# Deformable sampling on one core: the sum over 24 products moves from one VectorE reduction to a halving on VectorE and four adds on GpSimd, and VectorE makes one of the four one-hot blocks

## The chip, the core and the metric

The kernel runs on one core of a Trainium2 chip. The metric is device time in microseconds (us) of that core. The profile shows one execution; the span is the part of it that the trace covers.

## What is computed

The reference is a hybrid block: a group norm and a projection, a deformable attention over a 16x16 grid, a GEGLU feed-forward, a self-attention and a mixture of experts. The change lies in the sampling step of the deformable attention:

```
v   = value.reshape(bsz, L, NH, d)               # 4 images, L = 256 positions, 8 heads, d = 16
off = (query @ soff_w + soff_b)                  # 8 sample points (NP) per query and head
aw  = softmax(query @ attw_w + attw_b)           # a weight for each point
sampled = bilinear(v, px, py)                    # 4 corners each
out = einsum('bhqpd,bhqp->bqhd', sampled, aw)    # sum over the 8 points
```

## The kernel before, in words

The five engines run their own instruction lists, written by hand, and meet at counting semaphores. There is no planner: the order on an engine is the order of the text.

**Sampling.** For each head `i` (8 of them) and each half `u` of the query positions (2) there is one round, so 16 rounds. Four images are treated at once. In a round:

- `distances(i, u, c)` for c = 0 to 3 on TensorE (PE), line 1259: two matmuls of 512 columns write, for points 2c and 2c+1, a squared distance of each of 128 rows of the value table to the wanted row. Blocks 0 and 2 go to PSUM banks 0 and 1, blocks 1 and 3 to banks 2 and 3.
- `one_hots(i, u)` on ScalarE (ACT), line 574: Relu of one minus that distance turns each block of 1024 columns into a one-hot matrix in bf16 (`hot`). `hot` has a buffer for each u.
- `gather(i, u, b)` for images b = 0 to 3 on PE, line 1275: 24 matmuls of 48 columns each, the one-hot matrices as weights, fetch 8 points x 3 taps x 16 channels into PSUM banks 4 to 7. The first, `gather(i, u, 0)`, waits until all four one-hot blocks of its round are made.
- On VectorE (DVE), line 926: for each pair of images c (0 and 1) a multiplication of 768 columns by the weights `wk3` into `prod`; line 931: a reduction over the 24 products (8 points x 3 taps) of each channel into `msda`.

PE writes the distances of the next round between the gathers of the present one: `distances(next, 0)`, `gather(0)`, `distances(next, 1)`, `gather(1)`, and so on. Rounds run in a loop over heads, two rounds for each turn of the loop, on PE, ACT and DVE; the last head stands behind the loop.

`distances(i, u, c)` waits for the one-hot block that last used its banks. So block 3 waits until block 1 of the same round has been read, and, since PE works in order, everything behind it in PE's list waits as well.

**Ahead of the loop.** PE makes the four distance blocks of the first round in order. ACT makes one-hot block 0, then the exponentials of the softmax (line 587), then blocks 1, 2 and 3. DVE works off a list of its own before its loop: softmax sums, the tap weights `wk3` (line 909), and last the addition of a bias row to `t0_k` (line 913).

**GpSimd (POOL).** Once `wk3` is ready it splits the GEGLU weights and the query and key weights of the attention into a high and a low part: 16 instructions of 256 columns (lines 466 and 469), then one addition over 1024 columns (line 474). Then it has nothing to do until the sampling is over.

**Behind the loop.** PE does `residual()` and then transposes `msda` (line 1311), which waits for the last reductions. All that follows depends on that.

Of the kernel before, what the change touches and what calls it, by code (L numbers as in the profile page):

```python
# [19 lines left out]
P = 128  # L20
# [48 lines left out]
def build(nc, x, weights, vectors, rows, w1_t, w2_t, out):  # L69
    with ExitStack() as ctx:  # L70
        def sb(name, shape, dt=F32):
            return ctx.enter_context(nc.sbuf_tensor(name, shape, dt))
# [37 lines left out]
        sel_low = sb("sel_low", [P, 4, NP])  # L110
        minus_2j = sb("minus_2j", [P, P])

# [9 lines left out]
        def W(name):  # L122
            a, b = WAT[name]
            return w_sb[:, a:b]
# [9 lines left out]
        def tok(name):  # L134
# [70 lines left out]
        prod = hat_y[:, :, :, :].rearrange("q k t r -> q (k t r)").rearrange(  # L205
            "q (s b n d) -> q s b n d", s=2, b=2, d=DH)
        msda = sb("msda", [P, TILES, NH, DH])

# [69 lines left out]
        def sems(names):  # L278
            return [sem(n) for n in names.split()]
# [20 lines left out]
        terms_ready, terms_mm, terms_t_ready, wk3_ready = sems("terms_ready terms_mm terms_t_ready wk3_ready")  # L300
        dist_mm, hot_ready, g_ready, g_free, prod_free = sems("dist_mm hot_ready g_ready g_free prod_free")
        msda_mm, msda_c_ready, out_mm, t1_ready, t1_mm, t1_c_ready = sems(
            "msda_mm msda_c_ready out_mm t1_ready t1_mm t1_c_ready")
        geglu_parted, hn_h_ready, hn_l_ready, wqk_parted, z1_h_ready, z1_l_ready = sems(
# [58 lines left out]
        NMAX_ZEROED, V_ZEROED, ROUTE_ZEROED = 1, 2, 3  # L363
        HOT_CREDIT, G_CREDIT, FREE_CREDIT = 2, 3, 2
        CONSTS = 6
# [46 lines left out]
        def _(pool):  # L412
            nc.gpsimd.memset(one_c[:, :], 1.0)
            nc.gpsimd.memset(ident[:, :], 0.0).then_inc(pool_step, 1)
            nc.gpsimd.memset(group_mean[:, :], GROUPS / C).then_inc(pool_step, 1)
            nc.gpsimd.iota(minus_2j[:, :], pattern=[[-2, P]], base=0, channel_multiplier=0,
                           allow_small_or_imprecise_dtypes=True).then_inc(ramp_ready, 1)
# [39 lines left out]

            pool.wait_ge(ld_wc, 16)
            pool.wait_ge(wk3_ready, NK)
            wqk = w_sb[:, WAT["wq"][0]:WAT["wk"][1]]  # L460
            quarter = 2 * GE * P // 4
            for w, high, low, parted in ((W("geglu"), geglu_h, geglu_l, geglu_parted),
                                         (wqk, wqk_h[:, :], wqk_l[:, :], wqk_parted)):
                for n in range(4):
                    cols = slice(n * quarter, (n + 1) * quarter)
                    nc.gpsimd.tensor_tensor(high[:, cols], w[:, cols], one_c[:, 0:1].to_broadcast([P, quarter]),
                                            ALU.mult).then_inc(parted, 1)
                    pool.wait_ge(parted, 2 * n + 1)
                    nc.gpsimd.tensor_tensor(low[:, cols], w[:, cols], high[:, cols].bitcast(F32),
                                            ALU.subtract).then_inc(parted, 1)  # L470


            pool.wait_ge(fuse_ready, 3)
# [21 lines left out]
        def _(act):  # L495
# [15 lines left out]
            def selectors(which):  # L511
                for n in which:
                    h, p = n // NP, n % NP
                    at = 4 * NP * h + p
                    ins = nc.scalar.activation(sel[:, h, p, :], minus_2j[:, :], ACT.Identity,  # L515
                                               scale=ident[:, at:at + 1], bias=sel_low[:, h, p:p + 1])
                ins.then_inc(sel_ready, 1)
# [48 lines left out]

            def one_hots(i, u, which=range(NP // 2)):

                act.wait_ge(g_ready, 4 * i + 2 * u + 1)
                for c in which:
                    act.wait_ge(dist_mm, 8 * i + 4 * u + c + 1)
                    nc.scalar.activation(hot[:, u, 2 * c:2 * c + 2, :, :],  # L574
                                         ps[:, 2 * (c % 2):2 * (c % 2) + 2, :].rearrange("r p (b q) -> r p b q", b=B),
                                         ACT.Relu, scale=-1.0, bias=one_less_sq[:, 0:1]).then_inc(hot_ready, 1)

# [9 lines left out]
            nc.scalar.activation(aw[:, :, :], aw[:, :, :], ACT.Exp).then_inc(logit_exp, 1)  # L587
            one_hots(0, 0, range(1, 4))

# [152 lines left out]
        def _(dve):  # L742
# [42 lines left out]
            for k in range(NK):  # L785
# [3 lines left out]
            by_term = ident[:, :].rearrange("k (h c p) -> k h c p", h=4, c=4)  # L789
            nc.vector.tensor_tensor(sel_low[:, :, :], by_term[:, :, 1, :], by_term[:, :, 2, :],  # L790
                                    ALU.add).then_inc(sel_low_ready, 1)

# [49 lines left out]
            nc.vector.memset(gap[:, 2:3], 0.0).then_inc(g_free, FREE_CREDIT)  # L842
            nc.vector.memset(gap[:, 3:4], 0.0).then_inc(prod_free, FREE_CREDIT)

# [72 lines left out]

            with dve.Fori(0, NH) as i:
                for u in range(2):
                    for c in range(2):  # L920
                        dve.wait_ge(g_ready, 4 * i + 2 * u + c + 1 + G_CREDIT)

                        dve.wait_ge(prod_free, 4 * i + 2 * u + c + 1)
                        g = ps[:, 4 + 2 * c:6 + 2 * c, 0:NP * NK * DH].rearrange("q b (n d) -> q b n d", d=DH)
                        w = wk3[:, 4 * c + u:4 * c + u + 3:2, bass.ds(i * NP, NP), :].rearrange("q b p k -> q b (p k)")
                        nc.vector.tensor_tensor(prod[:, c, :, :, :], g,  # L926
                                                w.unsqueeze(3).to_broadcast([P, 2, NP * NK, DH]),
                                                ALU.mult).then_inc(g_free, 1)
                    for c in range(2):
                        dve.wait_ge(g_free, 4 * i + 2 * u + c + 1 + FREE_CREDIT)  # L930
                        nc.vector.tensor_reduce(msda[:, 4 * c + u:4 * c + u + 3:2, bass.ds(i, 1), :].rearrange(  # L931
                                                    "q b h d -> q b (h d)"),
                                                prod[:, c, :, :, :].rearrange("q b n d -> q b d n"),
                                                AX_X, ALU.add).then_inc(prod_free, 1)


# [221 lines left out]
        def _(pe):  # L1158
# [509 lines left out]
```

## Time and profile before

| | |
|---|---|
| median of 3 runs | 285.82 us (285.53 to 286.98) |
| the profiled execution's own time | 284.63 us |
| its span | 282.8 us |
| PE busy | 228.8 us (81%) |
| DVE busy | 210.1 us (74%) |
| ACT busy | 177.7 us (63%) |
| POOL busy | 50.0 us (18%) |
| sampling rounds, from the first gather to the last | 39.97 to 113.83 us of the span |

Busy times are sums over the whole span, which has several stages with different limits; what bounds the sampling has to be read inside its own stretch. All times below are us from the start of the span unless marked ns. The page of the profile says of itself that ends of matmuls are modelled and that spans on POOL are rough.

### The profile page before, as it was taken

The numbers are of one execution on the slowest core, as the hardware profiler recorded it, in microseconds if no ns is written. First come the engines' busy times: TensorE is split into PE (matmuls) and PEld (weight loads), VectorE is DVE, ScalarE is ACT, GpSimd is POOL, SyncE is SP. The second block draws the span as 40 slices with busy tenths as digits, with TensorE's granted clock in tenths as the row PEclk, the third lists the DMA queues.
The fourth block names the chain that finished last, engine by engine and source line by source line (L and its number), as shares of the span: only waits on it lengthen the run. The fifth ranks groups of instructions, "written<-read, shape, count | busy, mean of one in ns | idle before, by whom it ended". The sixth has DMA issues, their size and how long they took to land.

```text
span 282.8 us, 7527 instructions
## 1 busy us (share of the span) xinstructions
PE 228.8 (81%) x2908; PEld 158.0 (56%) x2908; DVE 210.1 (74%) x481; ACT 177.7 (63%) x260; POOL 50.0 (18%) x64
## 2 busy tenths in 40 slices
PE   0899469999999998769999568999876605999984
PEld 0579237676767677547989456666544404233352
DVE  4757887999999999874245877888747979697512
ACT  8678979898989897058343567566673232566510
POOL 7004939800000000010002000000000277500000
PEclk9999959999999999987999999999999555799999
DMA  6920000000000000690000000000009515130002
GB/s 144 378 94 2 1 0 2 0 2 0 0 0 0 0 0 2 241 351 4 0 3 0 0 0 2 2 0 2 1 2 370 234 48 163 44 112 2 0 2 74
DMA packets 8836, 16.15 MB, mean 57 GB/s; under 512 B 752, under 2 KB 5104, under 8 KB 8432
## 3 DMA queue, kind: packets, MB, share of 16 engines
q1 hardware_dynamic: 8304, 14.83, 15.0%
q0 software_dynamic: 512, 1.05, 1.2%
q8 instruction: 13, 0.21, 0.3%
q14 instruction: 7, 0.06, 0.1%
HBM read 12.73 MB, written 3.15 MB: 56 GB/s over the span
## 4 chain that ended last, share of the span: by engine, by line
PE 63%; DVE 12%; ACT 9%; issue 7%; DMA 4%; POOL 2%; SPq 1%; POOLq 0%; DVEq 0%; ACTq 0%
PE ps L1275 12%; PE ps L1259 9%; PE ps L1569 8%; ACT arena L574 3%; DVE t_k L972 3%; PE ps L1342 3%; PE ps L1425 2%; PE ps L1374 2%; POOL slot_rows L490 2%; PE ps L1386 2%; PE ps L1588 2%; PE ps L1163 2%; DMA r_sb<-in_rows 2%; PE ps L1332 2%; PE ps L1398 2%
## 5 line engine op out<-in xcount | busy, mean ns | idle before, releaser
L574 ACT ACTIVATE arena<-ps,one_less_sq 128x1024 bf16<-128x1024 f32 x64 | 68.7, 1114 | 7.3 <-PE ps L1259 7.0
L1275 PEld LDWEIGHTS ps<-arena 128*128 128x128 bf16 x1536 | 47.6, 96 | 19.7 <-issue 7.4
L1275 PE MATMUL ps<-arena 128*128 (+1 forms) x1536 | 50.4, 184 | 2.2 <-ACT arena L574 2.1
L1259 PE MATMUL ps<-wide,sel 128*128 (+1 forms) x128 | 39.2, 390 | 8.1 <-ACT arena L574 6.1
L931 DVE TENSOR_REDUCE msda<-wide 128x768 f32 x32 | 45.3, 1458 | 0.0
L926 DVE TENSOR_TENSOR wide<-ps,wide 128x768 f32<-128x768 f32 x32 | 29.8, 955 | 4.0 <-PE ps L1275 4.0
L490 POOL DMA_INDIRECT slot_rows<-nrm,slots x16 | 16.5, 1034 | 72.6 <-DVE slots L1067 68.0
L1569 PE MATMUL ps<-arena,w_sb 128*32 x48 | 23.3, 632 | 0.0
L972 DVE TENSOR_REDUCE t_k<-ps 128x2 f32<-128x512 f32 x32 | 20.5, 683 | 0.0
L643 ACT ACTIVATE wide<-ps 128x512 f32<-128x512 f32 x32 | 17.3, 595 | 1.4 <-PE ps L1410 1.3
L1574 PE MATMUL ps<-late,w_sb 128*32 128x512 f32 x80 | 16.5, 662 | 0.0
L1099 DVE COPY late<-arena 128x512 f32 x40 | 14.2, 425 | 2.2 <-issue 2.2
L947 DVE SCALAR_TENSOR_TENSOR wide<-ps,v_sb,wide 128x512 f32<-128x512 f32 x8 | 6.0, 751 | 12.8 <-ACT wide L616 12.8
L1259 PEld LDWEIGHTS ps<-wide,sel 128*128 (+1 forms) x128 | 8.8, 96 | 11.4 <-ACT arena L574 7.0
L965 DVE SCALAR_TENSOR_TENSOR xm<-ps,raw_by,xm 128x512 fp32r<-128x512 f32 x16 | 11.9, 748 | 3.7 <-ACT xm L632 1.9
L1569 PEld LDWEIGHTS ps<-arena,w_sb 128*32 128x32 f32 x48 | 5.4, 116 | 15.1 <-issue 15.1
L477 POOL MEMSET t_k<- 128x1024 f32 x1 | 1.0, 951 | 67.1 <-PE ps L1315 67.1
L515 ACT ACTIVATE sel<-minus_2j,sel_low,ident 128x128 bf16<-128x128 f32 x32 | 12.6, 479 | 0.0
L635 ACT ACTIVATE xm<-ps,high_by 128x512 fp32r<-128x512 f32 x8 | 5.5, 687 | 10.5 <-PE ps L1374 10.5
L737 ACT ACTIVATE sel<-ps 128x512 f32<-128x512 f32 x12 | 7.2, 598 | 7.0 <-PE ps L1574 7.0
L616 ACT ACTIVATE wide<-ps,v_sb 128x512 f32<-128x512 f32 x8 | 5.5, 691 | 8.6 <-PE ps L1332 8.6
L1163 PE MATMUL ps<-ident,nrm 128*128 128x128 f32 x32 | 8.5, 368 | 2.5 <-DVE nrm L777 2.5
(298 smaller groups left out, 497.3 us busy)
## 6 DMA issues: line engine op xcount, KB each, us to landing
arena<-in_w_t SPq DMA_DIRECT2D x1, 4096.0 KB, 15.0
wide<-in_w_t SPq DMA_DIRECT2D x1, 2048.0 KB, 8.0
slot_rows<-t_c SPq DMA_DIRECT2D x2, 768.0 KB, 9.9
wide<-in_w_t SPq DMA_DIRECT2D x1, 1536.0 KB, 11.3
late<-slot_rows SPq DMA_DIRECT2D x6, 256.0 KB, 3.6
w_sb<-in_weights SPq DMA_DIRECT2D x1, 1480.0 KB, 8.3
x_sb<-in_x SPq DMA_DIRECT2D x4, 128.0 KB, 2.3
wide<-in_w_t SPq DMA_DIRECT2D x1, 512.0 KB, 8.0
```

The lines of the kernel that those rows point to most:

```text
L490: nc.gpsimd.indirect_dma_start(out=scratch[h], out_offset=bass.IndirectOffsetOnAxis(ap=slots[:, c, t:t + 1], axis=0), in_=nrm[:, t, :], in ...
L574: nc.scalar.activation(hot[:, u, 2 * c:2 * c + 2, :, :], ps[:, 2 * (c % 2):2 * (c % 2) + 2, :].rearrange("r p (b q) -> r p b q", b=B), ACT ...
L643: nc.scalar.activation(prob_t[u % 2][:, i, :], ps[:, 2 + i % 2, :], ACT.Exp).then_inc(prob_ready, 1)
L926: nc.vector.tensor_tensor(prod[:, c, :, :, :], g, w.unsqueeze(3).to_broadcast([P, 2, NP * NK, DH]), ALU.mult).then_inc(g_free, 1)
L931: nc.vector.tensor_reduce(msda[:, 4 * c + u:4 * c + u + 3:2, bass.ds(i, 1), :].rearrange("q b h d -> q b (h d)"), prod[:, c, :, :, :].rear ...
L972: nc.vector.tensor_reduce(nmax[:, :, 2 * (u % 2) + i // 2, HROWS * (i % 2) + SPLIT], ps[:, i % 2, :].rearrange("q (t k) -> q t k", t=2), A ...
L1099: nc.vector.tensor_copy(staged_at[n % len(staged_at)], w1_sb[:, bass.ds(at[q][t % GROUP], 1), :].rearrange("d e f -> d (e f)")).then_inc(s ...
L1163: nc.tensor.transpose(ps[:, bank + t // 4, P * (t % 4):P * (t % 4) + P], nrm[:, t, :], ident[:, :]).then_inc(s["turned"], 1)
L1259: ins = nc.tensor.matmul(ps[:, 2 * (c % 2) + p % 2, :], sel[:, bass.ds(i % 4, 1), p, :].rearrange("k h j -> k (h j)"), terms_t[:, bass.ds( ...
L1275: ins = nc.tensor.matmul(ps[:, 4 + b, p * NK * DH:(p + 1) * NK * DH], hot[:, u, p, b, :], rhs, start=(s == 0), stop=(s == PARTS - 1))
L1569: nc.tensor.matmul(ps[0:GRAIN, 2 + t % 4, :], x_cols[:, t * P:t * P + GRAIN], w1_sb[:, bass.ds(at[j], 1), :].rearrange("d e f -> d (e f)"))
L1574: ins = nc.tensor.matmul(ps[GRAIN * q:GRAIN * (q + 1), 2 + t % 4, :], x_cols[:, t * P + GRAIN * q:t * P + GRAIN * (q + 1)], staged_at[entr ...
```

## The change

1. **Sum.** The reduction over 24 products is gone. DVE adds the two halves of each product (12 and 12) at once behind its multiplication, `halve(i, u, c)`, into a new buffer `part_sums`, which has a part for each u. GpSimd adds the remaining twelve down to one in four additions over all four images, `sums(step)`: 384, 192, 64 and 64 columns.
2. **Second one-hot block.** ACT makes blocks 0, 2 and 3 only. DVE makes block 1 from PSUM with one instruction (add, then maximum with 0), `second_one_hot`. For the first round this stands behind DVE's whole list ahead of the loop; in the rounds it stands ahead of the multiplications. To make it one such instruction, the distances come with the opposite sign (`twice_j` in place of `minus_2j`, the sign of `sel_low` turned).
3. **Order on GpSimd.** The 16 weight splits are parted: one ahead of the sums of each round.
4. **Waits.** `distances` of block 3 and `gather` of image 0 wait on the new semaphore `second_hot`; `gather` of image 0 waits for ACT's blocks as well. DVE's one-hot waits until both halvings of the round before are done. The final transposes wait for GpSimd's last sums.

```
-            for w, high, low, parted in ((W("geglu"), ...), (wqk, ...)):
-                for n in range(4):
-                    nc.gpsimd.tensor_tensor(high[:, cols], w[:, cols], one_c[:, 0:1].to_broadcast([P, quarter]), ALU.mult)
-                    pool.wait_ge(parted, 2 * n + 1)
-                    nc.gpsimd.tensor_tensor(low[:, cols], w[:, cols], high[:, cols].bitcast(F32), ALU.subtract)
+            def sums(step):
+                i, u = step // 2, step % 2
+                part = part_sums[:, u, :, :, :]
+                pool.wait_ge(halved, 2 * step + 2 + HALVED_CREDIT)
+                nc.gpsimd.tensor_tensor(part[:, :, 0:6, :], part[:, :, 0:6, :], part[:, :, 6:12, :], ALU.add)
+                pool.wait_ge(sum_step, 3 * step + 1)
+                nc.gpsimd.tensor_tensor(part[:, :, 0:3, :], part[:, :, 0:3, :], part[:, :, 3:6, :], ALU.add)
+                pool.wait_ge(sum_step, 3 * step + 2)
+                nc.gpsimd.tensor_tensor(part[:, :, 0, :], part[:, :, 0, :], part[:, :, 1, :], ALU.add)
+                pool.wait_ge(sum_step, 3 * step + 3)
+                nc.gpsimd.tensor_tensor(msda[:, u:u + 7:2, i, :], part[:, :, 0, :], part[:, :, 2, :],
+                                        ALU.add).then_inc(sums_ready, 1)
+            for step in range(2 * NH):
+                part_weights(step)
+                sums(step)
...
-            def one_hots(i, u, which=range(NP // 2)):
+            def one_hots(i, u, which=(0, 2, 3)):
...
-            one_hots(0, 0, range(1, 4))
+            one_hots(0, 0, (2, 3))
...
             dve.wait_ge(wk3_ready, NK)
-            with dve.Fori(0, NH) as i:
-                for u in range(2):
-                    for c in range(2):
-                        (multiply pair c)
-                    for c in range(2):
-                        nc.vector.tensor_reduce(msda[...], prod[:, c, :, :, :] as "q b d n", AX_X, ALU.add)
+            def second_one_hot(i, u):
+                dve.wait_ge(g_ready, 4 * i + 2 * u + 1)
+                dve.wait_ge(dist_mm, 8 * i + 4 * u + 2)
+                nc.vector.tensor_scalar(hot[:, u, 2:4, :, :], ps[:, 2:4, :], one_less_sq[:, 0:1], 0.0,
+                                        ALU.add, ALU.max).then_inc(second_hot, 1)
+            def halve(i, u, c):
+                dve.wait_ge(g_free, 4 * i + 2 * u + c + 1 + FREE_CREDIT)
+                nc.vector.tensor_tensor(part_sums[:, u, 2 * c:2 * c + 2, :, :], prod[:, c, :, 0:n, :],
+                                        prod[:, c, :, n:2 * n, :], ALU.add).then_inc(halved, 1)
+            def weighted(i, u, last):
+                (wait for both halvings of the round before)
+                second_one_hot(next round)
+                weigh(i, u, 0)
+                dve.wait_ge(sums_ready, 2 * i + u + 1)
+                halve(i, u, 0)
+                weigh(i, u, 1)
+                halve(i, u, 1)
+            second_one_hot(0, 0)
...
             def distances(i, u, c):
-                pe.wait_ge(hot_ready, 8 * i + 4 * u + c + 1)
+                if c == 3:
+                    pe.wait_ge(second_hot, 2 * i + u + 2)
+                else:
+                    pe.wait_ge(hot_ready, 6 * i + 3 * u + c + 1)
...
                 if b == 0:
-                    pe.wait_ge(hot_ready, 8 * i + 4 * u + 4 + HOT_CREDIT)
+                    pe.wait_ge(hot_ready, 6 * i + 3 * u + 3 + HOT_CREDIT)
+                    pe.wait_ge(second_hot, 2 * i + u + 2)
...
-                    pe.wait_ge(prod_free, 4 * NH + FREE_CREDIT)
+                    pe.wait_ge(sums_ready, 2 * NH + SUM_CREDIT)
```

## Rows read from the trace of the kernel before

**Rows 1.** Costliest groups: line, engine, tiles, count | busy us, mean ns | idle before.
```profile
L574 ACT ACTIVATE arena<-ps,one_less_sq 128x1024 bf16<-128x1024 f32 x64 | 68.7, 1114 | 7.3 <-PE ps L1259 7.0
L1275 PE MATMUL ps<-arena 128*128 (+1 forms) x1536 | 50.4, 184 | 2.2 <-ACT arena L574 2.1
L931 DVE TENSOR_REDUCE msda<-wide 128x768 f32 x32 | 45.3, 1458 | 0.0
L926 DVE TENSOR_TENSOR wide<-ps,wide 128x768 f32<-128x768 f32 x32 | 29.8, 955 | 4.0 <-PE ps L1275 4.0
```

**Rows 2.** Busy times by stretch: at the start, and one turn of the loop.
```profile
core 0: us, PE busy (x) PEld busy (x) DVE busy (x) ACT busy (x) POOL busy (x), PEclk, DMA share, GB/s
40.00:42.80 2.80, 2.80 (x49) 2.21 (x50) 2.62 (x4) 1.66 (x2) 1.11 (x1) 0.51 0.00 0
...
78.86:88.29 9.43, 9.02 (x210) 6.62 (x209) 9.04 (x9) 8.58 (x9) 0.00 (x0) 1.00 0.00 0
```

**Rows 3.** Chain that ended last, in order of time, 82 to 93 us.
```profile
82.22 1.12 ACT arena L574
83.34 0.12 issue
83.46 0.77 PE ps L1275 x24
84.23 0.43 PE ps L1259 x2
84.66 0.60 PE ps L1275 x24
...
87.33 0.23 issue
...
91.64 1.12 ACT arena L574
```

**Rows 4.** Timeline of one round: start us, us, engine, line.
```profile
83.01 0.96 DVE L926 TENSOR_TENSOR wide<-ps,wide 128x768 f32<-128x768 f32 x1 [0.39 <-PE ps L1275]
...
84.70 3.18 ACT L574 ACTIVATE arena<-ps,one_less_sq 128x1024 bf16<-128x1024 f32 x3 [0.27 <-PE ps L1259]
...
86.14 0.59 PE L1259 MATMUL ps<-wide,sel 128*128 x2
```

**Rows 5.** Timeline of the start of the rounds.
```profile
36.37 3.34 ACT L574 ACTIVATE arena<-ps,one_less_sq 128x1024 bf16<-128x1024 f32 x3
...
37.52 1.03 PE L1259 MATMUL ps<-wide,sel 128*128 128x512 bf16 x2 [2.34 <-ACT arena L574]
...
39.97 1.31 PE L1275 MATMUL ps<-arena 128*128 x24
...
41.43 1.20 DVE L913 TENSOR_TENSOR t_k<-t_k,fused 128x1024 f32<-128x1024 f32 x1
...
41.69 1.41 POOL L466 TENSOR_TENSOR xm<-w_sb,one_c 128x256 fp32r<-128x256 f32 x1 [4.47 <-DVE wide L909]
```

**Rows 6.** DVE groups near in kind to the new ones, shapes kept apart.
```profile
L965 DVE SCALAR_TENSOR_TENSOR xm<-ps,raw_by,xm 128x512 fp32r<-128x512 f32 x16 | 11.9, 748 | 3.7 <-ACT xm L632 1.9
...
L878 DVE TENSOR_TENSOR arena<-ps,arena 128x384 f32<-128x384 f32 x4 | 2.0, 546 | 0.4 <-ACT arena L557 0.4
```

**Rows 7.** PE's sequencer on the gather's line: count, ns min/median/max.
```profile
L1275 PEldq FUSED_REGOPS  x84: 46/46/70, 39.8 to 100.6; - x84
```

**Rows 8.** Two-input additions and the like on POOL, shapes kept apart.
```profile
L466 POOL TENSOR_TENSOR wqk_h<-w_sb,one_c 128x256 fp32r<-128x256 f32 x4 | 2.5, 616 | 0.0
...
L469 POOL TENSOR_TENSOR xm<-w_sb,xm 128x256 fp32r<-128x256 f32 x4 | 2.9, 729 | 0.3
...
L449 POOL TENSOR_TENSOR hat_x<-hat_x,t_k 128x512 f32<-128x512 f32 x1 | 1.3, 1269 | 0.1
```

**Rows 9.** Timeline of the end of the rounds.
```profile
111.26 2.57 PE L1275 MATMUL ps<-arena 128*128 128x48 bf16 x96 [0.61 <-ACT arena L574]
...
119.05 1.09 PE L1311 MATMUL ps<-ident,msda 128*128 128x128 f32 x8 [1.63 <-DVE msda L931]
```

**Rows 10.** Timeline at 31 us: DVE and POOL both read SBUF.
```profile
30.67 1.92 POOL L446 TENSOR_SCALAR wide<-y_rest 128x512 f32<-128x512 f32 x1
...
31.41 0.69 DVE L887 TENSOR_TENSOR aw<-proj,lmax 128x512 f32<-128x512 f32 x1
```

More of the change, by code:

```diff
@@ L514, in selectors @@
                     at = 4 * NP * h + p
-                    ins = nc.scalar.activation(sel[:, h, p, :], minus_2j[:, :], ACT.Identity,
+                    ins = nc.scalar.activation(sel[:, h, p, :], twice_j[:, :], ACT.Identity,
                                                scale=ident[:, at:at + 1], bias=sel_low[:, h, p:p + 1])
@@ L575, in one_hots @@
                                          ps[:, 2 * (c % 2):2 * (c % 2) + 2, :].rearrange("r p (b q) -> r p b q", b=B),
-                                         ACT.Relu, scale=-1.0, bias=one_less_sq[:, 0:1]).then_inc(hot_ready, 1)
+                                         ACT.Relu, bias=one_less_sq[:, 0:1]).then_inc(hot_ready, 1)
             act.wait_ge(val_r1, B)
@@ L789, in _ @@
             by_term = ident[:, :].rearrange("k (h c p) -> k h c p", h=4, c=4)
-            nc.vector.tensor_tensor(sel_low[:, :, :], by_term[:, :, 1, :], by_term[:, :, 2, :],
-                                    ALU.add).then_inc(sel_low_ready, 1)
+            nc.vector.scalar_tensor_tensor(out=sel_low[:, :, :], in0=by_term[:, :, 1, :], scalar=-1.0,
+                                           in1=by_term[:, :, 2, :], op0=ALU.mult, op1=ALU.subtract).then_inc(sel_low_ready, 1)
             for b in range(B):
@@ new lines, in second_one_hot, with weigh @@
+            def second_one_hot(i, u):
+                dve.wait_ge(g_ready, 4 * i + 2 * u + 1)
+                dve.wait_ge(dist_mm, 8 * i + 4 * u + 2)
+                nc.vector.tensor_scalar(hot[:, u, 2:4, :, :],
+                                        ps[:, 2:4, :].rearrange("r p (b q) -> r p b q", b=B),
+                                        one_less_sq[:, 0:1], 0.0, ALU.add, ALU.max).then_inc(second_hot, 1)
+            def weigh(i, u, c):
+                dve.wait_ge(g_ready, 4 * i + 2 * u + c + 1 + G_CREDIT)
+                g = ps[:, 4 + 2 * c:6 + 2 * c, 0:NP * NK * DH].rearrange("q b (n d) -> q b n d", d=DH)
+                w = wk3[:, 4 * c + u:4 * c + u + 3:2, bass.ds(i * NP, NP), :].rearrange("q b p k -> q b (p k)")
+                nc.vector.tensor_tensor(prod[:, c, :, :, :], g,
+                                        w.unsqueeze(3).to_broadcast([P, 2, NP * NK, DH]),
+                                        ALU.mult).then_inc(g_free, 1)
@@ new lines, in halve @@
+            def halve(i, u, c):
+                n = NP * NK // 2
+                dve.wait_ge(g_free, 4 * i + 2 * u + c + 1 + FREE_CREDIT)
+                nc.vector.tensor_tensor(part_sums[:, u, 2 * c:2 * c + 2, :, :], prod[:, c, :, 0:n, :], prod[:, c, :, n:2 * n, :],
+                                        ALU.add).then_inc(halved, 1)
+            def weighted(i, u, last):
+                if u == 0:
+                    dve.wait_ge(halved, 4 * i + HALVED_CREDIT)
+                else:
+                    dve.wait_ge(halved, 4 * i + 2 + HALVED_CREDIT)
+                if u == 0:
+                    second_one_hot(i, 1)
+                elif not last:
+                    second_one_hot(i + 1, 0)
+                weigh(i, u, 0)
[3 more added lines that the diff above has]
+                halve(i, u, 1)
@@ L937, in _ @@
+            second_one_hot(0, 0)
+            with dve.Fori(0, NH - 1) as i:
+                for u in range(2):
+                    weighted(i, u, False)
+            for u in range(2):
+                weighted(NH - 1, u, True)
             norm(lns["ln3"], 2, out_mm)
```

58 lines of the change are left out of this document (30 added, 28 removed).

## The prediction

> **What bounds the sampling now.** I read four views: the costliest groups, the busy times of one turn of the loop, the chain that ended last, and the timeline at both ends of the rounds. By the groups, DVE's reduction and ACT's one-hots look like the price of this stage [rows 1]; both are what the change lightens. The busy times of one turn (two rounds, 9.43 us) do not choose between them: PE 9.02, DVE 9.04, ACT 8.58 [rows 2]. The chain does [rows 3]. In 82 to 93 us it holds PE's work, PE's issue, and one ACT piece in each turn; DVE stands nowhere in it. The reader is to see three things there.
>
> First, a round with the ACT piece: the last distances of a round end, ACT starts one-hot block 3 at once (82.22), 1.12 us, 0.12 us of issue, and the gather starts at 83.46. ACT isn't late there: it starts as soon as PE has delivered. That block 3 is 1.12 us long counts; how many blocks ACT made before it doesn't. Second, if that wait were gone, PE would in the same place have a gather and a pair of distances to do, 0.60 + 0.43 = 1.03 us in the chain. The wait costs 1.24 - 1.03 = 0.21 us each turn. Third, the other round of the turn is PE alone, with 0.23 us of issue at the loop's end (87.33).
>
> DVE waits 0.39 us for PE once in a turn [rows 4]. It is nearly full but behind PE, not ahead of it. Only at the end is it late: the last gather ends at 111.26 + 2.57 = 113.83, and the transposes wait for the last reduction until 119.05 [rows 9].
>
> **ACT makes three blocks, not four.** 16 instructions of 1114 ns go [rows 1], 17.8 us of ACT. By the chain, what is left on the path is block 3 behind the last distances, and it stays. I take 0. The bound on the other side is PE with no wait at all: 0.21 x 8 = 1.7 us gained.
>
> **DVE's work in a round.** Removed: two reductions, 2 x 1.458 = 2.92 us. Added: two halvings of 384 columns. The same size from PSUM and SBUF took 0.546 [rows 6]; two are 1.09. Added too: block 1, 1024 columns from PSUM with a per-partition scalar. The slope is (955 - 546) / 384 = 1.065 ns a column [rows 1, 6]. L965, with such a scalar, is 748 ns at 512 columns [rows 6], so its fixed part is 748 - 545 = 203 ns, and block 1 is 1.09 + 0.20 = 1.29 us. ACT's 1.11 is the lower bound. A round on DVE goes from 2.92 + 1.91 = 4.83 to 1.29 + 1.91 + 1.09 = 4.29 us of instructions, 0.54 less. Hidden behind PE it is worth 0.
>
> **Is block 1 in time?** This is what DVE now owes PE. Count from the gather at 83.46. The second distances are there when ACT starts at 84.70; the fourth start at 86.14 [rows 4], and behind them stand the rest of PE's list. DVE's multiplication started at 83.01 and ends at 83.97. With hand-overs of 0.1 (the chain's issue is 0.12) the halving ends at 84.62, block 1 runs from 84.72 to 86.01, and PE has it at 86.11. That is in time by 0.03 us; with shorter hand-overs by 0.15. So 0 for this, but without reserve: each 0.1 us later costs 1.5 us over 15 rounds.
>
> **One wait more.** The first gather of a round waits on a second semaphore against a loop value. PE's sequencer takes 46 ns for such an operation [rows 7]. In the chain the gather follows its wait at once, so I add 0.04 x 15 = 0.6 us; the bounds are 0 and, at 0.12 each, 1.8.
>
> **The first round.** Here lies the price. ACT made block 1 of round 0 first in its group of three at 36.37, and PE started the fourth distances at 37.52 and the first gather at 39.97, 2.45 us later [rows 5]. DVE now makes this block, behind L913, which ends at 41.43 + 1.20 = 42.63 [rows 5]. Nothing in DVE's list ahead of it gets shorter or goes. Block 1 is then done at 42.63 + 1.29 = 43.92, and the fourth distances start at 43.95 or a little later: 6.4 us later than 37.52. Behind them in PE's list are the distances of round 1 and all gathers, so the first gather moves from 39.97 to 46.4. ACT's block 3 of round 0 waits for the same distances and ends before PE needs it. Nothing covers this: PE's first round in the trace follows its own pace, and the path through the rounds is PE's. I take +6.4, with 6.2 (block at ACT's duration) to 6.6. In the time before, TensorE ran at 1.2 GHz (granted 0.51) in 40.0 to 42.8, and at 2.4 GHz in the loop [rows 2], after having stood idle for 2.34 us ahead of 37.52 among others. It will now be idle longer, and it may stay at the lower level somewhat further into the rounds: 0 to 1.5 us more; I take 0.
>
> **GpSimd.** Its adds have 384, 192, 64 and 64 columns. From 729 ns at 256 and 1269 at 512 columns [rows 8], 2.11 ns a column and 0.19 fixed: 1.00 + 0.59 + 0.32 + 0.32 = 2.24 us, with four hand-overs of 0.1 about 2.65. One weight split is 0.62 to 0.73 [rows 8]. Together 3.3 us in a round of 4.7: it keeps up and has two buffers. The splits end later than now, but before the feed-forward that reads them, and the addition over 1024 columns behind them still ends ahead of its reader, PE's output of the feed-forward.
>
> **The end.** The last gather ends at G = 113.83 (unshifted). Multiplication 0.96, hand-over, halving 0.55: G + 1.7 = 115.5. GpSimd had the round before since about 112.4 (1.15 us behind the gather at 111.26, as counted above; the last round has no distances and takes 2.57 us): its sums 2.65 and a split 0.73 hold it to 115.8, or 116.3 if a halving holds it up. Then 2.65 us and a hand-over: transposes at 118.5 to 119.0 against 119.05 [rows 9]. I take -0.3.
>
> The turned sign costs nothing: `sel_low` and the ramp stay one instruction each, far ahead of their readers. The load of the expert weights, which SP starts behind the last gather, moves with the whole and is read much later.
>
> **Sum.** 6.4 + 0.6 - 0.3 = +6.7. The profiled execution, 284.63 before, should be about 291.3; the median of the runs shown lies 1.2 us above it, so 285.82 + 6.7 = 292.5.
>
> **Two engines on one memory.** A GpSimd instruction that began at 41.69 under L913, which has two SBUF inputs, took 1.41 us [rows 5] where 0.62 is usual [rows 8]; it ended 0.47 us behind L913. So the halving, also with two SBUF inputs, will hold GpSimd up, 2 x 0.55 us in a round at most, which fits: 3.3 + 1.1 = 4.4. The other way round, L887 with two SBUF inputs ran 0.69 us inside a GpSimd instruction of 1.92 us [rows 10] and wasn't held up: by the slope, 512 columns are 0.54 us and 0.14 fixed. The Trainium skill (SBUF — State Buffer, Who interferes with whom) says that whichever starts second blocks fully until the first has ended. Our trace agrees for GpSimd behind DVE and doesn't for DVE behind GpSimd at L887; by that rule the halvings would be held up too, and the sum would be that of the second case below.
>
> **The cases.**
> (1) Forecast, 0.62: start +6.4, rounds unchanged, 290.5 to 294.5.
> (2) Halvings are held up by GpSimd's adds, 0.18. The adds run from about 1.2 us behind the gather's start for 3.3 us, so the first halving, at 3.4, meets them. Held up by half an instruction to a whole one, 0.3 to 1.0 us, it pushes the second multiplication, the second halving and block 1, which has no reserve: 0.1 to 0.4 us a round, 1.5 to 6 us, 294 to 299. For it: the row at 41.69 shows that the two do collide. Against: L887.
> (3) ACT's relief does help, 0.10: the wait of 0.21 in each turn goes, with the best end: 6.4 - 1.7 - 0.6 = +4.1, 289.9; with part of the start hidden, 288.
> (4) The other side, 0.06: DVE, not PE, sets the pace. Then each round is 0.54 shorter, 8.6 us, against 6.4 at the start: 283.6. It decides from 0.4 us a round on. DVE's 9.04 of 9.43 speaks for it; that it waits 0.39 for PE and is in no piece of the chain, against.
> (5) The lower clock lasts longer, 0.04: 294 to 296.
>
> The range 289 to 298 leaves out the far ends of (2) and (3), and (4). A measurement of this kernel tells 0.5% (1.4 us) from no change. Slower by more: (1), (2), (5) and nearly all of (3), 0.92; faster 0.05; within 0.03.
>
> **What the changed profile would show.** Right: PE idle from about 36 to 43.9 waiting for DVE's block 1 in front of the fourth distances; first gather near 46.4; turns of the loop at 9.4 to 9.5 us; ACT with 3 blocks and over 2 us idle a turn; DVE's one-hot near 1.3 us; four adds and a split of 3.3 us on GpSimd; transposes about 5 us behind the last gather. Wrong: a first gather before 43 us; turns of 8.9 us or less (case 4), or of 9.7 and more with PE waiting for DVE's one-hot in front of the fourth distances (case 2); halvings clearly over 0.55 us.

## The result, and the profile after

The changed kernel takes 299.59 us (median of 4 runs, 297.49 to 299.77), the kernel before 285.67 us beside it (4 runs): ratio 1.0453, 95% interval 1.0397 to 1.051. Slower, as forecast, but by 13.9 us where 6.7 were forecast, and outside the range of 289 to 298. Measured again (f3), the changed kernel came out at 298.25 us (ratio 1.0365, 1.0297 to 1.0432). Ratios leave out runs more than 1.5% above the fastest of the same kernel, which show a lower granted clock; in e4 and g2 most runs are such, the profiled ones too, so these two have no ratio.

The profiled execution took 299.55 us, its span is 297.8: 15.0 more than before. First the costliest groups of the page (line, engine, tiles, count, busy us, mean ns, idle before), to be read against [rows 1, 6, 8].

```profile
L600 ACT ACTIVATE arena<-ps,one_less_sq 128x1024 bf16<-128x1024 f32 x48 | 52.6, 1112 | 31.9 <-PE ps L1318 31.9
...
L1318 PE MATMUL ps<-wide,sel 128*128 (+1 forms) x128 | 39.9, 398 | 13.3 <-DVE arena L950 8.2
...
L959 DVE TENSOR_TENSOR wide<-ps,wide 128x768 f32<-128x768 f32 x32 | 30.4, 951 | 1.1 <-PE ps L1335 1.0
L950 DVE TENSOR_SCALAR arena<-ps,one_less_sq 128x1024 bf16<-128x1024 f32 x16 | 20.5, 1283 | 10.4 <-PE ps L1318 10.4
L482 POOL TENSOR_TENSOR wide<-wide 128x384 f32<-128x384 f32 x16 | 16.0, 998 | 32.2 <-DVE wide L967 32.2
...
L967 DVE TENSOR_TENSOR wide<-wide 128x384 f32<-128x384 f32 x32 | 19.1, 598 | 2.2
```

The new instructions have about the forecast sizes: one-hot on DVE 1.283 us, first add on GpSimd 0.998. ACT's relief has become 31.9 us of idle time. And PE's distances now waited 8.2 us for DVE's one-hot, in one place. The timeline of that place, the changed kernel, against [rows 5]:

```profile
42.06 1.20 DVE L941 TENSOR_TENSOR t_k<-t_k,fused 128x1024 f32<-128x1024 f32 x1
43.19 1.27 DVE L950 TENSOR_SCALAR arena<-ps,one_less_sq 128x1024 bf16<-128x1024 f32 x1
44.52 1.89 PE L1318 MATMUL ps<-wide,sel 128*128 128x512 bf16 x4 [8.23 <-DVE arena L950]
...
47.07 1.34 PE L1335 MATMUL ps<-arena 128*128 x24 [0.66 <-ACT arena L600]
```

The fourth distances stand behind 8.23 us of waiting, and the first gather is at 47.07 instead of 39.97. The chain of a turn in the rounds, the changed kernel, against [rows 3]:

```profile
82.48 0.77 PE ps L1335 x24
...
85.32 0.52 PE ps L1318 x2
85.83 0.60 PE ps L1335 x24
...
87.22 0.12 issue
87.35 0.97 PE ps L1335 x24
...
90.86 1.12 ACT arena L600
...
92.10 0.77 PE ps L1335 x24
```

A turn is 92.10 - 82.48 = 9.62 us where it was 9.43. Two pieces are new in kind: 0.12 us of issue ahead of the gather at the loop's start, and fourth distances of 0.52 us where a pair takes 0.43. What stands ahead of these, by the timeline of the changed kernel:

```profile
83.81 1.28 DVE L950 TENSOR_SCALAR arena<-ps,one_less_sq 128x1024 bf16<-128x1024 f32 x1 [0.25 <-PE ps L1318]
...
85.23 0.60 PE L1318 MATMUL ps<-wide,sel 128*128 x2
```

DVE had waited 0.25 us for PE's second distances before it began block 1, and PE began the fourth distances 0.14 us behind its end. The timeline of the end, the changed kernel, against [rows 9]:

```profile
119.58 0.61 POOL L470 TENSOR_TENSOR wqk_h<-w_sb,one_c 128x256 fp32r<-128x256 f32 x1
...
119.59 1.02 DVE L967 TENSOR_TENSOR wide<-wide 128x384 f32<-128x384 f32 x1
...
120.49 2.57 PE L1335 MATMUL ps<-arena 128*128 128x48 bf16 x96 [0.61 <-ACT arena L600]
...
123.16 0.56 DVE L967 TENSOR_TENSOR wide<-wide 128x384 f32<-128x384 f32 x1
...
123.22 0.95 POOL L485 TENSOR_TENSOR wide<-wide 128x192 f32<-128x192 f32 x1
...
128.51 1.09 PE L1371 MATMUL ps<-ident,msda 128*128 128x128 f32 x8 [1.85 <-POOL msda L490]
```

The transposes start at 128.51, 9.46 us later than the 119.05 of before. That leaves 15.0 - 9.46 = 5.5 us that arise behind the sampling, in stages that the diff does not touch. The busy times by stretch show two of them; the columns are those of [rows 2]. Changed kernel: the attention, and the expert stage.

```profile
163.43:210.84 47.41, 40.27 (x333) 30.17 (x331) 36.45 (x71) 28.67 (x50) 1.91 (x3) 0.89 0.00 1
...
252.68:283.92 31.24, 29.05 (x238) 8.91 (x241) 20.90 (x61) 15.78 (x28) 3.57 (x4) 0.94 0.12 35
```

Kernel before, the same two stretches:

```profile
153.66:198.55 44.89, 36.57 (x332) 27.20 (x331) 36.28 (x71) 28.68 (x50) 1.91 (x3) 1.00 0.00 1
...
240.67:268.88 28.21, 28.21 (x237) 8.68 (x240) 20.71 (x60) 16.15 (x28) 3.43 (x4) 0.94 0.13 39
```

The attention runs at a granted clock of 0.89 instead of 1.00: the same matmuls keep PE busy for 40.27 us instead of 36.57, and the stage takes 2.5 us longer. TensorE was at 1.2 GHz from 174.6 on for 10.2 us. The expert stage is 3.0 us longer with the mean clock unchanged (0.94), but the low stretch lies elsewhere: before, it is at the start of the stage (240.67 to 244.1); in the changed kernel nearly all of it comes later, from 259.9 to 263.3. Ahead of that, ACT and DVE stand still for over 3 us, by the timeline of the changed kernel:

```profile
256.14 0.60 ACT L753 ACTIVATE w_sb<-ps 128x512 f32<-128x512 f32 x1 [3.66 <-remote]
...
259.13 2.77 DVE L1155 COPY late<-arena 128x512 f32 x8 [3.39 <-remote]
```

"Remote" means that the profile saw no instruction of this core that released them.

### The profile page after: what moved, and what is told of

It is laid out like the page before. It is cut to its first block, busy times and chain, and to the rows that moved or that the text cites. A ratio compares the mean times of both kernels' runs of the same rounds, so it can differ in the third digit from the quotient of the medians.

```text
span 297.8 us, 7579 instructions
## 1 busy us (share of the span) xinstructions
PE 236.4 (79%) x2908; PEld 164.8 (55%) x2908; DVE 206.1 (69%) x499; ACT 161.1 (54%) x244; POOL 88.8 (30%) x128
## 4 chain that ended last, share of the span: by engine, by line
PE 63%; DVE 14%; ACT 10%; issue 5%; POOL 2%; another core or an unknown queue 2%; DMA 2%; SPq 1%; DVEq 1%; ACTq 0%
PE ps L1335 12%; PE ps L1318 8%; PE ps L1629 6%; ACT arena L600 4%; DVE t_k L1028 3%; PE ps L1434 3%; PE ps L1402 2%; PE ps L1219 2%; PE ps L1485 2%; PE ps L1446 2%; PE ps L1648 2%; PE ps L1458 2%; DMA r_sb<-in_rows 2%; PE ps L1392 1%
## 5 line engine op out<-in xcount | busy, mean ns | idle before, releaser
L600 ACT ACTIVATE arena<-ps,one_less_sq 128x1024 bf16<-128x1024 f32 x48 | 52.6, 1112 | 31.9 <-PE ps L1318 31.9
L1335 PEld LDWEIGHTS ps<-arena 128*128 128x128 bf16 x1536 | 48.5, 97 | 20.1 <-issue 9.4
L1335 PE MATMUL ps<-arena 128*128 (+1 forms) x1536 | 51.2, 185 | 3.5 <-ACT arena L600 2.8
L950 DVE TENSOR_SCALAR arena<-ps,one_less_sq 128x1024 bf16<-128x1024 f32 x16 | 20.5, 1283 | 10.4 <-PE ps L1318 10.4
L482 POOL TENSOR_TENSOR wide<-wide 128x384 f32<-128x384 f32 x16 | 16.0, 998 | 32.2 <-DVE wide L967 32.2
L967 DVE TENSOR_TENSOR wide<-wide 128x384 f32<-128x384 f32 x32 | 19.1, 598 | 2.2
L1318 PEld LDWEIGHTS ps<-wide,sel 128*128 (+1 forms) x128 | 9.8, 97 | 17.5 <-DVE arena L950 9.1
L541 ACT ACTIVATE sel<-twice_j,sel_low,ident 128x128 bf16<-128x128 f32 x32 | 12.6, 479 | 0.0
L780 DVE BATCH_NORM_STATS2 ln_st<-ps 128x6 f32<-128x128 f32 x24 | 5.3, 283 | 10.1 <-PE ps L1375 6.9
L1434 PE MATMUL ps<-z_h,wqk_h 128*128 128x256 f32 x32 | 11.4, 356 | 0.0
```

Source lines behind the costliest of these rows:

```text
L482: nc.gpsimd.tensor_tensor(part[:, :, 0:6, :], part[:, :, 0:6, :], part[:, :, 6:12, :], ALU.add).then_inc(sum_step, 1)
L600: nc.scalar.activation(hot[:, u, 2 * c:2 * c + 2, :, :], ps[:, 2 * (c % 2):2 * (c % 2) + 2, :].rearrange("r p (b q) -> r p b q", b=B), ACT ...
L950: nc.vector.tensor_scalar(hot[:, u, 2:4, :, :], ps[:, 2:4, :].rearrange("r p (b q) -> r p b q", b=B), one_less_sq[:, 0:1], 0.0, ALU.add, A ...
L967: nc.vector.tensor_tensor(part_sums[:, u, 2 * c:2 * c + 2, :, :], prod[:, c, :, 0:n, :], prod[:, c, :, n:2 * n, :], ALU.add).then_inc(halv ...
L1318: ins = nc.tensor.matmul(ps[:, 2 * (c % 2) + p % 2, :], sel[:, bass.ds(i % 4, 1), p, :].rearrange("k h j -> k (h j)"), terms_t[:, bass.ds( ...
L1335: ins = nc.tensor.matmul(ps[:, 4 + b, p * NK * DH:(p + 1) * NK * DH], hot[:, u, p, b, :], rhs, start=(s == 0), stop=(s == PARTS - 1))
```

## The experiments

Each was run beside the kernel before, and a ratio compares it with that; the kernel before itself took 287.0 us beside e1 to e4, 288.64 beside f1 to f4 and 288.24 beside g1 to g3 (medians; one run of 719.49 us, beside g1 to g3, is out of all ratios). Beside the time I read three marks of each profile: the first gather, the transposes, and what is left of the span behind the transposes. The first two give the price in the sampling; the third tells what came from elsewhere.

**e1: the first round's block 1 back on ACT.** The rounds keep the change.

```diff
 ACT, ahead of one_hots(0, 0, (2, 3)):
+    act.wait_ge(dist_mm, 2)
+    nc.scalar.activation(hot[:, 0, 2:4], ps[:, 2:4], ACT.Relu, bias=one_less_sq).then_inc(second_hot, 1)
 DVE, ahead of its loop:
-    second_one_hot(0, 0)
```

> One-hot block 1 of round 0 alone goes back to ScalarE; all else as in the changed kernel. Theory A (the start): the first gather returns from 47.1 to about 40.0 us, the turns of the loop stay at 9.62 us, the transposes of msda come at about 120.7 (119.05 before, plus 0.2 us for each of 7 turns); if the 5.5 us lost behind the transposes were a consequence of the late start they go too and the time is 286.5 to 288; if they belong to the new code they stay and it is 291 to 293. Rival B (the rounds themselves, VectorE's one-hot and GpSimd's sums, make the cost): the time stays above 294.

290.19 us, ratio 1.015 (1.0095 to 1.0204). First gather 40.47, transposes 121.43, so 6.60 and 7.08 us ahead of the changed kernel's. One edit at one place holds most of the price in the sampling. The turn stays at 9.63 us.

**e2: the sums alone.** As e1, and ACT makes block 1 in every round; the second wait stays.

```diff
-    def one_hots(i, u, which=(0, 2, 3)):
+    def one_hots(i, u, which=(0, 1, 2, 3)):
+        ready = second_hot if c == 1 else hot_ready
 DVE:
-    second_one_hot(next round)
```

> ScalarE makes all four one-hot blocks again; only the halvings, GpSimd's sums and the parted weight splits remain. Theory A: the first gather near 40.0 us, turns of 9.43 to 9.5 us (TensorE and the fourth block set the pace, VectorE has 3.0 us of work in a round of 4.7), transposes at 118.5 to 119.2, time 285 to 287. Rival C (GpSimd and VectorE in each other's way on SBUF lengthen the rounds): turns of 9.6 us or more, 288 or more.

287.51 us (10 runs), ratio 1.0026 (0.9981 to 1.0071), level with the kernel before and not faster. First gather 40.87, transposes 120.80, turn 9.54 us. In its chain the fourth distances take 0.43 us again, and the 0.12 us of issue is still there; the chain of e2:

```profile
88.20 0.43 PE ps L1319 x2
...
90.02 0.12 issue
90.15 0.97 PE ps L1336 x24
```

**e3: the one-hot alone.** As e1, but DVE sums by its old reductions and GpSimd splits the weights in one piece.

```diff
-    halve(i, u, c) and GpSimd's sums(step)
+    nc.vector.tensor_reduce(msda[...], prod[:, c], AX_X, ALU.add)   # c = 0, 1
```

> VectorE makes block 1 of each round but the first (that one on ScalarE) and reduces over 24 products as in the kernel before; GpSimd does the weight splits in one piece at the start. Work of VectorE in a round by instructions: 1.29 + 1.91 + 2.92 = 6.1 us, less 0.3 of overlap. Theory A: VectorE becomes the bound, a turn takes about 11.6 us, the time is 300 to 306. Rival D (what bounds the round is ScalarE's four blocks): turns of 9.4 us or less.

310.94 us (one run), a turn of about 12.7 us where 11.6 had been expected. The timeline of e3 shows why:

```profile
74.37 1.27 DVE L952 TENSOR_SCALAR arena<-ps,one_less_sq 128x1024 bf16<-128x1024 f32 x1
...
75.78 0.60 PE L1319 MATMUL ps<-wide,sel 128*128 x2 [1.72 <-DVE arena L952]
```

PE waits 1.72 us for DVE's block, and DVE in turn waits for PE behind it (17.38 us busy of 20.00). So the two parts of the change are not independent: the sums are what makes room for the one-hot on DVE.

**e4: the kernel before, started late.** An unused memset of 0.91 us on DVE, at the place of the new one-hot, holds back the fourth distances of the first round.

```diff
+    nc.vector.memset(late[:, 0:1024], 0.0).then_inc(dve_consts, 1)   # ahead of DVE's loop
 def distances(i, u, c):
+    if c == 3:
+        pe.wait_ge(dve_consts, 3)
```

> The kernel before, in which TensorE's fourth distances of round 0 wait until VectorE has done the t0_k addition (L913) and one memset of 1024 columns behind it: a late start and nothing else. Theory A: first gather about 6.2 us later, at 46.2; turns stay 9.43. What it tells: if the lower TensorE clock at the start and the loss of 5.5 us behind the transposes follow from the late start, the time is 294 to 299; if they don't, it is 291.5 to 293. Rival B (the rounds make the cost): at most 293 too, so that the rounds would have to show the rest.

297.69 us (median of 4; the fastest 292.47, against 285.33 for the fastest of before beside it). The timeline of e4 shows the changed kernel's start with the old code:

```profile
43.19 0.91 DVE L918 MEMSET late<- 128x1024 f32 x1 [0.16 <-issue]
...
46.61 1.32 PE L1276 MATMUL ps<-arena 128*128 x24 [0.56 <-ACT arena L574]
...
126.65 1.09 PE L1314 MATMUL ps<-ident,msda 128*128 128x128 f32 x8 [1.63 <-DVE msda L932]
```

The transposes are 7.6 us later than before: 6.64 from the start, 0.94 from a first round of 6.72 us instead of 5.78, at a mean granted clock of 0.63 instead of 0.76. The attention of this kernel is slow as well; the busy times of e4:

```profile
161.73:209.47 47.74, 39.40 (x332) 29.06 (x331) 36.38 (x71) 28.67 (x50) 1.91 (x3) 0.93 0.00 1
```

So the slow attention needs no line of the change. It doesn't always come with the late start either: the fastest run of e4, at a mean clock of 0.924 where the profiled one had 0.896, is 7.1 us above the fastest of before, about what the later transposes alone give.

**f1, f2: TensorE filled with useless matmuls ahead of the fourth distances,** in the changed kernel (f1: 12 and 24) and in the one before (f2: 12 and 7). This was to show whether the idle time at the start brings the low clock.

```diff
+    def fill(n):
+        for k in range(n):
+            nc.tensor.matmul(ps[:, 4 + k % 4, :], sel[:, 0, 0, :], terms_t[:, 0, 0:HALF])
 def distances(0, 0, c):
+    if c == 2: fill(12)
+    if c == 3: fill(24)      # 7 in f2
```

> The changed kernel, with 36 matmuls of 512 columns without use on TensorE in the time in which it waits ahead of the rounds (12 in front of the third distances, 24 in front of the fourth), so that it isn't idle there. The late start stays. Theory E (the lower clock in the first rounds follows from the idle time ahead of them): the granted clock stays near 1.00 from 36 to 52, the first gather comes at 46 or a little earlier, the first round is about 4.8 us and not 6.6, gain 1.5 to 2.5 us: 295 to 298. If the low stretch at 174 to 185 us, in the attention, hangs on that idle time too, it goes and 2.5 us more with it. Rival: the low stretches hang on nothing ahead of the rounds; the gain is the first round alone.

> The kernel before with 19 such matmuls in its own two waits ahead of the rounds (12 and 7). Theory E: the clock stays up, the first round takes about 4.8 us in place of 5.78, the start of the gathers isn't later than 40.0: 0.5 to 1.5 us faster than before. Rival: VectorE, whose own list ends at 42.6, holds the first rounds back and nothing is gained, or the matmuls delay the fourth distances: same to 1 us slower.

f1: 300.09 us, ratio 1.0426 (1.0367 to 1.0485): nothing gained. The timeline of f1 shows the second filling and what PE did next:

```profile
35.59 5.34 PE L1361 MATMUL ps<-wide,sel 128*128 128x512 bf16 x24
...
44.43 1.89 PE L1318 MATMUL ps<-wide,sel 128*128 128x512 bf16 x4 [3.49 <-DVE arena L950]
```

The busy times of f1 at the start, in two neighbouring stretches:

```profile
34.00:43.90 9.90, 5.96 (x27) 2.46 (x26) 8.44 (x12) 4.01 (x5) 5.13 (x3) 1.00 0.00 0
...
43.90:50.00 6.10, 4.70 (x54) 2.79 (x56) 1.26 (x2) 2.12 (x2) 0.00 (x0) 0.54 0.00 0
```

The filling was too short: it ended at 40.93, PE then stood idle for 3.49 us until DVE's block was there, and the clock, 1.00 until then, fell to 1.2 GHz at 44.3. The first round took 6.44 us (6.59 in the changed kernel). The attention is at 47.49. So f1 doesn't test a start without idle time. f2 does: there PE never waited longer than 1.0 us ahead of the rounds, and the clock stayed at 1.00 through the whole first round, which took 4.79 us instead of 5.78. f2 took 289.31 us, ratio 1.0046 (1.0003 to 1.0089), not the 0.5 to 1.5 us less that were expected: what is left behind the transposes is 166.7 us against 163.8 before, with 3.4 us at 1.2 GHz in its attention.

**f3: the changed kernel again,** beside f1, f2 and f4.

> The changed kernel once more, unchanged, for its spread and its low stretches of the clock. If the loss of 5.5 us behind the transposes belongs to it, the times are again 297 to 300 and the profile again has a stretch at the lower clock in the attention (170 to 190 us); if it was chance, some executions come at 292 to 294.

298.25 us. First gather 46.99, transposes 128.34, attention 47.42; but the expert stage 29.6 instead of 31.24.

**f4: all weight splits ahead of all sums** on GpSimd; else the changed kernel.

```diff
 for step in range(2 * NH):
     part_weights(step)
+for step in range(2 * NH):
     sums(step)
```

> The changed kernel with all 16 weight splits on GpSimd ahead of the first sums, as before, in place of one ahead of the sums of each round. Theory A: GpSimd keeps up with or without them, they cost nothing in the rounds: turns of 9.62 us as in the changed kernel, same time within 1 us; at the end the last sums no longer stand behind a split, 0.3 to 0.8 us gained there. Rival C (GpSimd's reads lengthen VectorE's halvings and through them the rounds): turns go to 9.5 us or less, 1 us or more faster.

296.32 us, ratio 1.0282 (1.0231 to 1.0333), 1.9 us less than f3. Turns stay at 9.6 to 9.7 us. The transposes are at 127.58, 0.76 ahead of f3's; the attention had the full clock, by the busy times of f4:

```profile
162.22:207.08 44.86, 36.55 (x333) 27.19 (x331) 36.28 (x71) 28.66 (x50) 1.91 (x3) 1.00 0.00 1
```

All four runs of f4 have a mean granted clock of 0.918, and the eight of the changed kernel 0.891 to 0.908. Here the changed way of sampling has an undisturbed attention, as before's code had a disturbed one in e4.

**g1: the first block stays on DVE, but moved up** to where DVE waits for the exponentials.

```diff
+second_one_hot(0, 0)
 dve.wait_ge(logit_exp, 1)
 ...
-second_one_hot(0, 0)      # ahead of the loop
```

> The changed kernel with one move: VectorE makes block 1 of round 0 not behind its list ahead of the loop but in the 1.3 us in which it waits for ScalarE's exponentials (at about 35.2 us). Theory A: PE's fourth distances of round 0 start at 37.5 to 38.6, the first gather at 40 to 41, the rest as in the run with that block on ScalarE: turns of 9.62 us, transposes at 121.0 to 121.6, time 289.5 to 291.5. Rival: the block delays the softmax chain on VectorE by as much as it takes, so that VectorE's list ends at 43.3 and the loop's first rounds wait for it: transposes above 122.

292.24 us, ratio 1.0202 (1.0114 to 1.029). The timeline of g1:

```profile
35.58 1.27 DVE L927 TENSOR_SCALAR arena<-ps,one_less_sq 128x1024 bf16<-128x1024 f32 x1
...
36.98 0.69 DVE L933 TENSOR_REDUCE lsum<-aw 128x64 f32<-128x512 f32 x1
...
39.45 1.32 PE L1335 MATMUL ps<-arena 128*128 x24
```

The block fits into a wait that DVE had anyway; the first gather is even 0.52 us earlier than before. Its first round, though, took 6.92 us at a mean granted clock of 0.63, so the transposes, at 121.29, are only 0.14 us ahead of e1's. So it was the place in DVE's list, not the engine, that cost 6.6 us.

**g2: the sums alone, with the waits of before.** e2 with all four blocks on one semaphore.

```diff
-    pe.wait_ge(hot_ready, 6 * i + 3 * u + 3 + HOT_CREDIT)
-    pe.wait_ge(second_hot, 2 * i + u + 2)
+    pe.wait_ge(hot_ready, 8 * i + 4 * u + 4 + HOT_CREDIT)
```

> Sums on GpSimd as in the changed kernel, all one-hot blocks on ScalarE, and TensorE's waits as in the kernel before (one semaphore, no second wait ahead of the first gather). If the 0.1 us a turn of the run with the sums alone (9.54 against 9.43) is the second wait, turns are 9.43 to 9.45 here; if it is the sums, 9.54. Time within 0.5% of the kernel before either way, 0.5 to 1 us under the run with the sums alone.

Median 292.02 us of 6 runs, one of them 285.75 at a clock of 0.928. The turn is 9.43 us again, and the transposes are at 119.80. The chain of g2 at the place of the second wait:

```profile
88.44 0.23 issue
88.67 0.60 PE ps L1312 x2
89.27 0.94 PE ps L1328 x24
```

There is no issue ahead of the gather. Its attention, though, is the slowest of all, with 17 us at 1.2 GHz (the profiled run took 293.84 us); the busy times of g2:

```profile
154.81:205.71 50.90, 42.59 (x332) 31.91 (x331) 36.57 (x71) 28.71 (x50) 1.91 (x3) 0.83 0.00 1
```

**g3: the changed kernel, with the transposes held** by an unused memset on GpSimd behind the last sums, to see what another time of arrival does to the attention.

```diff
+nc.gpsimd.memset(late[:, 6 * T:6 * T + 1536], 0.0).then_inc(sums_ready, 1)
-pe.wait_ge(sums_ready, 2 * NH + SUM_CREDIT)
+pe.wait_ge(sums_ready, 2 * NH + SUM_CREDIT + 1)
```

> The changed kernel with one memset of 1536 columns on GpSimd between the last sums and the transposes: everything behind the sampling comes about 1.4 us later, nothing else is altered. Theory F (the stretch at the lower clock in the attention hangs on when the attention starts against the clock's own stretches, not on the sampling's code): the attention's length changes, as it did in the run with the weights first, where it came 1.1 us earlier and took 44.9 and not 47.4 us. Rival G (the changed sampling always brings it): 47.4 us again, and the time is 1.4 us above the changed kernel, 299 to 300.

298.31 us, ratio 1.037 (1.0292 to 1.0448). Transposes 129.02, attention 46.38 with 3.4 us at 1.2 GHz, where f3, arriving 0.7 us earlier, had 47.42 with 10.2. The memset alone took 1.38 us, and the result is level with f3.

## Why the prediction was wrong in size

The sampling can be parted with the profiles of g2, e2, e1 and the changed kernel, since each adds one thing. All in us:

| kernel | first gather | first round | from there to the last group of gathers | from there to the transposes | adds |
|---|---|---|---|---|---|
| before | 39.97 | 5.78 | 65.51 | 7.79 | |
| g2 | 40.65 | 6.21 | 65.51 | 7.43 | sums on GpSimd: 0 in the rounds, -0.36 at the end |
| e2 | 40.87 | 6.35 | 66.17 | 7.41 | second wait: +0.66 in the rounds |
| e1 | 40.47 | 6.08 | 66.85 | 8.03 | block 1 on DVE in the rounds: +0.68 there, +0.62 at the end |
| after | 47.07 | 6.59 | 66.83 | 8.02 | the first block 1 on DVE: +6.60 ahead, +0.51 in the first round |

The first round is the time from the first gather to the first gather of the next round. These are single profiles; the first gather alone moves by up to 0.9 us between kernels with nearly the same work ahead of it.

**The start: right.** Forecast +6.4 with 6.2 to 6.6; measured 6.20, 6.42 and 6.60 against e2, g2 and e1. Of the 7.10 us against the profile before, 0.6 is DVE's list coming later as a whole (its addition to `t_k` at 42.06, 41.43 before [rows 5]). Most of that needs no line of the change: e4, with the code of before ahead of this addition, has it at 41.82. One detail was wrong: ACT's block 3 did not end before PE needed it, and the first gather waited 0.66 us for it. g1 shows the mechanism: block 1 was late because of what stood in front of it.

**The second wait: right.** Forecast 0.6, measured 0.66. It shows only where the loop starts, 0.11 us a turn (9.54 in e2, 9.43 in g2), and not in each of its two rounds.

**Block 1 in time: the step that failed inside the sampling.** "In time by 0.03 us" was 0.09 too late in one round of two: fourth distances of 0.52 us where a pair takes 0.43, and turns of 9.63 (e1) against 9.54 (e2). The reckoning had block 1 start 1.26 us behind the gather, when the halving was through. In the timeline it started 1.33 us behind (83.81 against 82.48), and PE's second distances released it, which the reckoning had as ready before. Its end was handed over in 0.14 us. The rounds lose 0.7 us by it, the rate that the forecast had given (0.1 us for each round in which it is late) over half of the rounds. The forecast had taken 0. It had not priced that DVE, with block 1 ahead of its multiplications, is late at the end of the rounds too: there the transposes wait for DVE and GpSimd, and e1 loses 0.62 us against e2.

**The end: right without block 1, wrong with it.** Forecast -0.3. The sums alone give -0.36 (g2) and -0.38 (e2). With block 1 it is +0.23 (8.02 against 7.79): the sums of the round before the last start at 122.14, 1.65 us behind the last group of gathers and not 1.15, for their halving was held at 119.59; the two adds behind took 0.95 and 0.71 us where 0.59 and 0.32 are usual; and the split at 125.32 stood in front of the last sums. f4 takes the splits away from there and comes to 7.34.

**ACT's relief: right.** It was taken as 0, and 31.9 us of idle time behind PE agree with it; case (3) is out. Case (4) is out with turns of 9.62 us. That is between the signs named, 9.4 to 9.5 for right and 9.7 and more for case (2).

**The halvings held up: real, but cheap.** Case (2) forecast 0.3 to 1.0 us for each. Over all 32 they took 598 ns in the mean against 546 forecast, and g2, which has these adds too, has turns of 9.43 us, as before. Single ones are held: the one at 119.59 took 1.02 us, behind an instruction of GpSimd that had begun 0.01 us earlier. The Trainium skill (SBUF — State Buffer, Who interferes with whom) says that the one that comes second is blocked until the first has ended. The rows agree both ways round, but for a start of 0.14 us that overlaps: 119.58 + 0.61 + 0.56 is 120.75, and the halving ended at 120.61; 123.16 + 0.56 + 0.59 is 124.31, and the add ended at 124.17. [Rows 10] did not agree, and what is different there was not tried.

**The clock at the start: mis-sized, within its bounds.** "It may stay at the lower level somewhat further into the rounds: 0 to 1.5 us more; I take 0." From the first gather to that of the next round before took 5.78 us, g2 6.21, the changed kernel 6.59, e4 6.72, at mean granted clocks of 0.76, 0.70, 0.65 and 0.63 in the same order. So this term is 0.8 us, 0.4 of it in g2 already. The profile of f2 shows that the idle time ahead of the rounds brings it: filled, with waits of at most 1.0 us left, the first round ran at 1.00 and took 4.79 us. In f1 an idle 3.49 us was left, and the clock fell at its end.

**What lies behind the sampling: the step that cost the range.** The sum went on from the transposes to the end as if all behind them only moved; no case priced anything else there. In the profiles it was 5.5 of the 15.0 us; by the medians it is 4.9 of the 13.9. What is left of the span behind the transposes, in us:

| before | f2 | e2 | e1, e3, f4 | g1, f3 | e4 | after, f1 | g3 | g2 |
|---|---|---|---|---|---|---|---|---|
| 163.8 | 166.7 | 165.0 | 166.5 | 167.8 to 167.9 | 169.0 | 169.3 to 169.4 | 170.2 | 172.3 |

(Worked out as span minus transposes.) The profile before was the shortest of all thirteen. For the attention the cause is shown as far as the clock: it takes 44.9 us where the granted clock is 1.00 (before, e2, e3, f4), and 46.4 to 50.9 with 3.4 to 17 us at 1.2 GHz. It is shown that the changed code is not needed for it (e4, f2) and does not force it (f4). Not shown is what decides: f3 and g3 differ by when the stage is reached and have different low stretches, but no order by time of arrival fits all of them, and the mean granted clocks of whole runs suggest that such stretches are more frequent with the change. The changed kernel was at 0.908 or below in all eight of its runs, where f4, with the same late start and no low stretch in the attention, was at 0.918. The kernel before was at 0.889 or 0.890 in four of the 36 runs beside the experiments, with 293.89 to 296.37 us; these have no profile. The Trainium skill (TensorE: Matmul & The Clock Gate, The HAM clock gate) says that 1.2 GHz is the default and that activity of the engine lifts it. The two levels agree with the profiles, 0.50 and 1.00 in such stretches; but PE does the same work in this stage in all thirteen, so the rule alone does not say why some have a low stretch.

For the expert stage (28.2 before; 29.2 to 29.6 in e1, e2, e4, f2, f3, g1 and g2; 31.1 to 31.3 after, in e3, f1, f4 and g3) the cause stays open. f3 and the changed kernel are one and the same, with 29.6 and 31.2. The stall on ACT, 3.66 us in the changed kernel, has no releaser in the trace and is in f3 too (4.36 us), so it alone doesn't part the two. What does is the place of a low stretch: the five profiles of about 31.2 have one of 3.4 us that begins behind the stall, and in the other eight the stage is at 1.2 GHz only in its first 3.4 to 4.2 us. That the two go together is shown; which brings which is not.

In short, by the table about 9 us of the price lie in the sampling: 6.6 the start, 1.3 block 1 in the rounds and at the end, 0.7 the wait, 0.8 the clock in the first round, less 0.4 by the sums. That is 2.3 more than the 6.7 forecast. The rest of the 13.9 lies in stages behind whose code is unchanged and whose time moves from profile to profile, with the change and without it; how much of it the change brings on is not shown. No version beat the kernel before. The best, e2, is level (1.0026), and so is the fastest run of g2.

## What to carry to other kernels

When an operation goes to another engine, price its first instance by itself: what stands ahead of it in that engine's list is the price, and a place in an existing wait (g1) can take nearly all of it away. Relief for an engine whose last block is gated by another was worth nothing here, and an instruction "in time by 0.03 us" has to be given a price: here it was late by 0.09. A late start may be dearer than itself: the stages behind it were not of fixed length here, so look at several profiles of the same kernel before you take their length for granted, and give it a term and a range in the sum.

## What was not expected of the hardware

- The attention stage took 44.9 to 50.9 us in thirteen profiles with the same code of that stage, 0 to 17 us of it at 1.2 GHz.
- Filling TensorE's waits ahead of the first gather in the kernel before (f2) kept 2.4 GHz through the first round, 4.79 us instead of 5.78, but the whole came out level (1.0046). In f1 the filling ended at 40.93, 3.49 us early, and the clock fell to 1.2 GHz at 44.3.
- Two-input instructions of DVE and GpSimd, both from SBUF, that began within 0.01 us of each other at 119.58 took 0.61 and 1.02 us, so the second one ended nearly at the sum of both.
- A second wait on a loop value ahead of a matmul cost 0.11 us in a turn of two rounds.
